# Moving GpSimd's copy of the next unit's weights ahead of the scatter in a routed expert kernel

## What is computed

```python
scores = softmax(xn @ wg_router.T)              # 32 experts
topk_w, topk_idx = top_k(scores, 6)             # six experts for each token
topk_w = topk_w / (sum(topk_w) + 1e-20)
# each expert e gathers its tokens:
ye = (silu(xe @ w_gate[e]) * (xe @ w_up[e])) @ w_down[e]      # 512 -> 352 -> 512
y  = sum over a token's experts of topk_w * ye
y += (silu(xn @ ws_gate) * (xn @ ws_up)) @ ws_down            # shared expert, width 704
```

## Time and profile before

| what | value |
|---|---|
| median of 3 runs | 938.03 us (935.12 to 940.43) |
| the profiled execution | 941.67 us |
| its span, first to last instruction | 939.7 us |
| busy PE, PEld | 906.4 us (96%), 803.1 us (85%) |
| busy DVE, ACT, POOL | 644.5 us, 517.5 us, 394.0 us |
| mean granted TensorE clock | 0.994 of full |
| moved by DMA | 191.28 MB, mean 204 GB/s |

### The profile page before, as it was taken

How to read it: one execution, slowest core, us unless ns; L and a number is a source line. 1 busy time by engine, 2 the same in 40 slices (tenths; PEclk the granted TensorE clock), 3 DMA queues, 4 the chain that set the end, 5 groups by cost and what they waited for, 6 DMA issues and landing times.

```text
span 939.7 us, 13872 instructions
## 1 busy us (share of the span) xinstructions
PE 906.4 (96%) x4428; PEld 803.1 (85%) x4428; DVE 644.5 (69%) x1138; ACT 517.5 (55%) x876; POOL 394.0 (42%) x318
## 2 busy tenths in 40 slices
PE   5799999999999999999999999999999999999997
PEld 4668888888887899999999989989889999898986
DVE  6888876655447776777776677866767667658665
ACT  7884441212135656666656666755656566557561
POOL 3001000010301666566666755756456546555321
PEclk9899999999999999999999999999999999999999
DMA  8552164223544998988999898999999999999865
GB/s 305 199 168 90 54 222 139 90 60 102 168 135 112 316 244 222 272 232 231 226 229 228 228 266 220 236 230 232 280 229 239 251 263 244 222 240 285 191 120 122
DMA packets 127722, 191.28 MB, mean 204 GB/s; under 512 B 16384, under 2 KB 73488, under 8 KB 127392
## 3 DMA queue, kind: packets, MB, share of 16 engines
q1 hardware_dynamic: 102480, 132.56, 44.9%
q0 software_dynamic: 23856, 57.29, 29.6%
q10 hardware_dynamic: 1312, 0.53, 0.2%
HBM read 121.16 MB, written 42.61 MB: 174 GB/s over the span
## 4 chain that ended last, share of the span: by engine, by line
PE 39%; DMA 16%; SPq 13%; POOL 11%; issue 9%; ACT 5%; DVE 5%; POOLq 1%; ACTq 1%; DVEq 0%
SPq L509 13%; DMA xnT<-xn_rows,ids 9%; PE p_gu L1231 7%; PE p_gu L1233 7%; PE p_gu L1232 7%; POOL out L776 7%; DMA xnT<-xnT 5%; PE p_y L1231 4%; PE p_y L1232 4%; PE p_y L1233 4%; POOL xnT L762 2%; ACT w_hi L850 2%; POOL wts L788 2%; DMA xnT<-xn_rows 1%; DVE xT_raw L1894 1%
## 5 line engine op out<-in xcount | busy, mean ns | idle before, releaser
L776 POOL DMA_INDIRECT out<-rows,ids x112 | 208.0, 1857 | 203.5 <-ACT rows L850 179.2
L1231 PE MATMUL p_gu<-xT_hi,w_hi 128*128 128x512 f32 (+12 forms) x816 | 287.6, 352 | 2.0 <-DVE xT_lo L1517 2.0
L1233 PE MATMUL p_gu<-xT_hi,w_lo 128*128 128x512 f32 (+12 forms) x816 | 287.6, 352 | 0.0
L1232 PE MATMUL p_gu<-xT_lo,w_hi 128*128 128x512 f32 (+12 forms) x816 | 287.5, 352 | 0.0
L762 POOL DMA_INDIRECT xnT<-xn_rows,ids x112 | 133.4, 1191 | 127.2 <-DVE xT_lo L1517 45.8
L1517 DVE TENSOR_TENSOR w_lo<-raw,w_hi 128x1024 fp32r<-128x1024 f32 (+2 forms) x148 | 173.8, 1177 | 5.8 <-ACT w_hi L850 5.8
L1231 PEld LDWEIGHTS p_gu<-xT_hi,w_hi 128*128 128x128 f32 x816 | 153.8, 188 | 14.0 <-DVE xT_lo L1517 2.5
L1232 PEld LDWEIGHTS p_gu<-xT_lo,w_hi 128*128 128x128 f32 x816 | 153.9, 189 | 11.5
L1233 PEld LDWEIGHTS p_gu<-xT_hi,w_lo 128*128 128x128 f32 x816 | 153.8, 188 | 7.8
L850 ACT ACTIVATE w_hi<-raw 128x1024 fp32r<-128x1024 f32 (+2 forms) x148 | 151.5, 1027 | 5.2 <-PE p_gu L1233 4.8
L1231 PE MATMUL p_y<-w_hi,hT_hi 128*128 128x512 f32 (+1 forms) x368 | 145.7, 396 | 8.5 <-ACT rows L850 6.8
(11 more groups left out here) (209 smaller groups left out, 1079.3 us busy)
## 6 DMA issues: line engine op xcount, KB each, us to landing
raw<-L_ffn_w_gate SPq DMA_DIRECT2D x32, 704.0 KB, 5.7
raw<-L_ffn_w_up SPq DMA_DIRECT2D x32, 704.0 KB, 7.5
xnT<-xnT SPq DMA_DIRECT2D x424, 48.0 KB
raw<-L_ffn_w_down SPq DMA_DIRECT2D x32, 512.0 KB, 8.7
raw<-L_ffn_w_down SPq DMA_DIRECT2D x32, 192.0 KB, 9.6
xring<-out SPq DMA_DIRECT2D x20, 256.0 KB, 3.4
out<-xring SPq DMA_DIRECT2D x20, 256.0 KB, 2.4
xnT<-xnT SPq DMA_DIRECT2D x80, 64.0 KB
```

What stands on the lines that cost most here:

```text
L776: pool.indirect_dma_start(out=out[:, :], in_=y_sb[t][0:n, :], in_offset=None, out_offset=bass.IndirectOffsetOnAxis(ap=ids[0:n, col:col + 1 ...
L1231: t_.matmul(dst, stat[0], mov[0], start=first, stop=False)
L1232: t_.matmul(dst, stat[0], mov[1], start=False, stop=False)
L1233: return t_.matmul(dst, stat[1], mov[0], start=False, stop=last)
```

## The change

The copy of a unit's weights no longer stands at the head of its own iteration. The first one (SH) is done ahead of the loop, and each iteration, behind its gather and ahead of its scatter, copies those of the next unit.

```diff
             gather(SH)
             gather(SH + 1)
+            weights(SH)
             for u in range(SH, CLOSE):
-                weights(u)
                 if u + 2 < CLOSE:
                     pool.wait_ge(s_xt, TURNED + blocks_before(u + 1))
                     pool.wait_ge(s_wu, weights_ready(u))
                     gather(u + 2)
+                if u + 1 < CLOSE:
+                    weights(u + 1)
                 if u == SH + 1:
                     for i in range(4):
                         pool.wait_ge(s_sst[i], 16 * TPB)
```

## The result

The changed kernel took 934.12 us (median of 10 runs, 930.83 to 934.84), the kernel before 939.57 us (10 runs, 935.12 to 944.51). The ratio is 0.9931, with a 95% interval of 0.9909 to 0.9954. That is 6.5 us of 939.6, between 4 and 9, faster by over 0.5% by its middle. A later group of runs measured the same kernel again and gave 0.9944 (0.9924 to 0.9963), so 5.3 us. The forecast was 930 us (8.1 us) in a range of 924.5 to 938.5; it was counted from 938.03 us, the median of the kernel before at that time, and from 939.57 us the same 8.1 us would give 931.5. One execution of the kernel before that took 2364.73 us, in the group of e5 to e8, is left out of the ratios.

The account below looks back on a forecast made before the run. PE was taken to wait for a two-unit loop through the data path: 10.8 us, less 2.7 us that DMA takes back, leaves 8.1 us off 941.67, so 933.6, scaled to 930 us; range 924.5 to 938.5.

Parts of the forecast that it names:

- What bounds the kernel: PE, busy 96%, runs neck and neck with the data path and waits at the first down chunk once in two units.
- the pot: PE's idle time ahead of p_y over 504 to 905 us, all the change can win: 10.8 us.
- The loop: Two-unit chain: scatter, weights copy, gather, landing, quarter DMAs, transposes, ACT's rows, next scatter; a small-unit round takes 36.9 us.
- two views: PE's idle time at p_y over 504 to 905 us: 7.7 us by matmuls, 13.9 us by weight loads.
- What the move takes out: Between scatter and gather in POOL's list: the copy and its 0.89 us semaphore go, so the gather starts earlier.
- two prices: Gain per late round at the gather: 1.8 us by start time, 1.07 us if DVE's w_lo holds its first DMA.
- late round: Rounds of one parity, some ten, whose quarters DVE awaits about 3 us and which make PE wait; the other parity is punctual.
- What is put in: The copy between gather and scatter, covered by POOL's wait for ACT (8.00 and 4.16 us in small units): cost 0.
- What DMA takes back: DMA engines, 0.96 busy over 684 to 869 us, stretch landings: a quarter of the pot, 2.7 us, is lost.
- signs of being wrong: PE's idle gone but time unchanged; same waits with gathers landing later than 7.1 us behind issue; new waits at punctual transposes.
- The saving is eaten: Rival, chance 0.30: w_lo's hold or DMA transfers absorb the earlier gather before PE; 0 to 4.5 us won, about 936 us.
- Slower, in the way of the punctual round's quarters: Rival, chance 0.08: the earlier gather delays the other parity's quarters, awaited by DVE with 0.17 us to spare; 943 us.

Follow-up runs that it names:

- e5: Changed kernel with DVE's w_lo subtraction of the down part moved behind the unit's last hT_lo, some 4 us later: 933.03 us, ratio 0.9912.
- e8: Changed kernel with the gather of u+4 issued ahead of the last block of the scatter of u: 986.75 us, ratio 1.047.
- e9: Changed kernel with the first two rows of the unit before put ahead of xT_hi in ACT's list: 929.11 us, ratio 0.9881.
- e10: Kernel before, with ACT's first two rows of the unit before moved ahead of xT_hi: 930.31 us, ratio 0.9885.
- e1: Changed kernel with the copy back between scatter and gather, but no semaphore to wait for: 935.23 us, ratio 0.9932.
- e2: Changed kernel with two small POOL memsets, each waited for, added behind the gather: 934.23 us, ratio 0.9925.
- e6: Kernel before, loading half the weight bytes (a quarter of w_gate and w_up from the third expert on): 933.52 us, ratio 0.9917.
- e7: Changed kernel, loading half the weight bytes (a quarter of w_gate and w_up from the third expert on): 931.14 us, ratio 0.9882.
- e11: The changed kernel measured again, without any edit, in a later group: 935.48 us, ratio 0.9944.
- e4: Changed kernel with DVE's w_lo down part subtracted in three instructions of 512 columns instead of one of 1536: 934.6 us, ratio 0.9917.

## Why the prediction was right

**What bounds the kernel, and the pot.** Right. The loop was named from the chain and from DVE's waits for quarters, and PE's loss put at 10.8 us as the middle of two views. e9 and e10 take that loss away and gain 0.0119 and 0.0115 of 939.99 us, 11.2 and 10.8 us, each within some 2.2 us. That the middle of 7.7 and 13.9 us comes so near is luck in part: the two views are 6 us apart, and no run says which share of each is lost.

**What the move takes out.** The place was right; of the two prices, 1.8 us by the timeline alone and 1.07 us with the hold by w_lo, the second is nearer (3.21 us between scatter's end and first gather DMA's end before, 2.62 us in the changed kernel and 2.46 us in e1, so 0.6 to 0.75 us off in the late round, less still than 1.07). But the quarters wait for the last gather DMA, and the second one is slowed too (1.36 us in place of 1.04 in the rounds shown): the last one starts 0.65 us sooner on the mean, not 1.07. The sum took this saving only as enough to empty the pot, ten rounds against 10.8 us.

**What is put in.** Right: scatters still wait 192.4 us for ACT in all, as the waits of POOL in the changed kernel say, and the copy behind the gather costs nothing (e2: nor do two memsets more, 0.28 us and their semaphores).

```profile
POOL out L776 <- ACT rows L852: 192.4, 32, 10.9
```

**What DMA takes back.** This is the term that was mis-sized. I took a quarter of the pot, 2.7 us; the measured gains of 6.5 and 5.3 us leave 4 to 6 us of it. The middle of the profile has it at 4.15 us. It sits where it was expected, in the small units: in 684 to 869 us PE still stands 185 - 182.81 = 2.2 of the 2.7 us. e6 and e7 show that the transfers have a part in it. By the table the landing takes back all of the 0.65 us by which the last gather DMA starts sooner, and not a quarter; one of my signs of being wrong, waits in the same places with gathers that land more than 7.1 us behind their issue, came in part (7.11 us on the mean and 6.93 in e11, from 6.40). The round is shorter by 0.7 us because scatters are no longer held by w_lo (0.4 us) and because less is waited for behind the quarters; ten such rounds are 7 us. The first of these was not in the sum. So the place of the gain, PE's waits, was right, and the size came in part by another way than the one counted: that much is luck. Why the scatters come clear of w_lo, and how late rounds and punctual ones share the rest, the runs don't tell.

**The rivals.** "The saving is eaten" described what happened to 40 to 50% of the pot, and to the gather's landing as a whole. By its time, 933.5 to 938 us, the measured 934.12 us lies within it; by its gain, 0 to 4.5 us, the measured 6.5 and 5.3 us lie above it. "Slower, in the way of the punctual round's quarters" didn't come: the waits for quarters over 320 to 905 us fell. In the changed kernel:

```profile
DVE xT_raw L1896 <- DMA xnT<-xnT: 22.5, 14, 3.2
```

Before they were 35.2 us in 18 waits. There was a new wait of PE, in the first large units, which I had not looked for (in e11 it is 0.80 and 1.10 us); PE's timeline of the changed kernel has it:

```profile
344.50 0.50 PE L1233 MATMUL p_y<-w_hi,hT_hi 128*128 128x512 f32 x1 [0.55 <-ACT rows L852]
```

That a gather can do much harm to what follows it in its queue is what e8 shows, but for the scatter, not for the quarters.

## What to carry to other kernels

When an engine that is busy 96% of the time waits now and then for a loop through other engines, add up those waits: that sum is all that any shortening of the loop can win. Here its two views were 7.7 and 13.9 us, and taking the waits away won about 11. Then check that a part of the loop that starts sooner also ends sooner: here the gathers' landings gave the time back. Look also for the place where an in-order list puts something late ahead of something ready; moving two rows in ACT's list won about twice what shortening the loop did. And ahead of moving a DMA up, ask what will stand behind it in its queue, and who waits for that to land.

## What was not expected of the hardware

- An indirect DMA of POOL beside a 1.75 us DVE subtraction with two SBUF inputs ended 0.97 us behind it in the rows shown of before, changed and split form alike, also where it had started 0.4 us ahead of the subtraction (e4). In e5 the third gather DMA ended 0.90 us behind it. Three subtractions of 512 columns, back to back, held it as one of 1536 did, up to 3.27 us.
- A POOL copy of 3 columns took 0.19 us in the free, and 1.76 us beside such a subtraction; what it lost in the late round of e1, the next indirect DMA had not to lose again.
- A scatter block issued behind three gather blocks of the same queue took 9.34 us to land (e8), and the kernel 4.7% longer.
- Gathers that were issued sooner behind a scatter took longer to land: 6.40 us before, 7.11 us in the changed kernel, 7.69 us in e5 (means of 18).
- Loading half the weight bytes shortened the kernel by 7.8 us without one instruction less, though PE was already busy for 393 of 401 us.
